# A graph network's first layer: ScalarE's and TensorE's inputs to a batch's tables are placed earlier, VectorE's readings of them later

## The reference, cut to what matters

```python
# N = 6250 nodes, 206250 edges (src, dst) sorted by dst, x is 6250 x 128
def _mean_agg(x, src, dst, n):
    msg_sum = segment_sum(x[src], dst, num_segments=n)
    cnt = segment_sum(ones, dst, num_segments=n)
    return msg_sum / maximum(cnt, 1.0)
def _sage_conv(x, src, dst, Wl, bl, Wr):
    return _mean_agg(x, src, dst, n) @ Wl.T + bl + x @ Wr.T
h = maximum(layernorm(x), 0)
h = relu(batch_norm(_sage_conv(h, ..., Wl0, bl0, Wr0)))   # 128 -> 256, "layer 0"
h = relu(batch_norm(_sage_conv(h, ..., Wl1, bl1, Wr1)))   # 256 -> 256, "layer 1"
h = log_softmax(_sage_conv(h, ..., Wl2, bl2, Wr2))        # 256 -> 128, "layer 2"
return x + h
```

## Time and profile before

| | us |
|---|---|
| median of 3 runs | 1572.43 (1569.44 to 1576.12) |
| the profiled execution | 1564.77 |
| its span in the trace | 1563.0 |
| mean granted TensorE clock in it | 0.953 |
| TensorE busy (matmuls) | 1338.6 |
| VectorE / ScalarE / GpSimd busy | 597.6 / 524.1 / 575.3 |

### The profile page before, as it was taken

One profiled execution on the slowest core, in us unless ns is written; L12 is line 12 of the kernel. 1 busy time (PEld: TensorE's weight loads), 2 busy tenths in 40 slices (PEclk: granted clock), 3 DMA queues, 4 the chain that ended last, 5 costly groups with the idle time before them and its releaser, 6 DMA issues.

```text
span 1563.0 us, 36182 instructions
## 1 busy us (share of the span) xinstructions
PE 1338.6 (86%) x16035; PEld 872.4 (56%) x16035; DVE 597.6 (38%) x1108; ACT 524.1 (34%) x848; POOL 575.3 (37%) x586
## 2 busy tenths in 40 slices
PE   1467787768777678899999999999999899999997
PEld 1366676657666667776544444444444774444445
DVE  6966656656476667521201111110210321212213
ACT  4875675657656557634200000000000150000001
POOL 4323132140221310000066666666666004666650
PEclk9988988889899989999999999999999999999999
DMA  5243434352524424413666666676664369888993
GB/s 156 89 160 123 169 112 167 104 182 87 190 103 173 180 89 178 168 40 130 211 227 211 222 213 220 211 241 232 204 228 150 86 207 315 319 300 308 330 320 103
DMA packets 92007, 291.45 MB, mean 186 GB/s; under 512 B 17538, under 2 KB 53012, under 8 KB 88612
## 3 DMA queue, kind: packets, MB, share of 16 engines
q1 hardware_dynamic: 63596, 228.73, 40.9%
q0 software_dynamic: 21824, 55.44, 11.6%
q10 hardware_dynamic: 6424, 4.88, 1.0%
HBM read 197.78 MB, written 91.22 MB: 185 GB/s over the span
## 4 chain that ended last, share of the span: by engine, by line
PE 66%; DVE 10%; issue 9%; POOL 6%; DMA 4%; ACT 4%; ACTq 0%; DVEq 0%; SPq 0%; POOLq 0%
PE bank L1638 25%; PE bank L1215 12%; PE cells L1638 12%; PE cells L1205 4%; DVE hots L889 3%; PE bank L1883 3%; DVE parts L889 2%; DMA hots<-table,src_i 2%; POOL hots L519 2%; PE cells L1250 2%; PE cells L1704 2%; PE bank L1641 2%; ACT junk L606 2%; POOL parts L482 2%; POOL parts L492 1%
## 5 line engine op out<-in xcount | busy, mean ns | idle before, releaser
L519 POOL DMA_INDIRECT hots<-table,src_i x444 | 420.6, 947 | 440.9 <-DMA table<-parts 206.1
L1638 PE MATMUL bank<-ring,parts 128*128 128x500 f16 x2058 | 461.4, 374 | 0.0
L1215 PE MATMUL bank<-ring,parts 64*128 64x250 f16 x4900 | 346.5, 285 | 115.9 <-DVE agm L900 112.1
L658 ACT CAST ring<-cells 128x980 f16<-128x980 f32 (+1 forms) x325 | 337.6, 1054 | 210.1 <-PE cells L1205 203.8
L1215 PEld LDWEIGHTS bank<-ring,parts 64*128 64x128 f16 x4900 | 249.7, 100 | 140.4 <-issue 118.7
L1638 PEld LDWEIGHTS bank<-ring,parts 128*128 128x128 f16 x2058 | 192.3, 96 | 224.8 <-issue 11.3
L1638 PE MATMUL cells<-ring,parts 128*128 128x500 f16 (+1 forms) x980 | 215.9, 373 | 0.0
L889 DVE TENSOR_TENSOR hots<-iotas,tab 128x2560 f16<-128x2560 f16 (+1 forms) x210 | 198.5, 1002 | 9.5 <-ACT tab L622 8.2
L729 ACT ACTIVATE agmg<-cells,isp 128x124 f32<-128x124 f32 x20 | 7.3, 365 | 470.0 <-PE cells L1259 470.0
L1638 PEld LDWEIGHTS cells<-ring,parts 128*128 128x128 f16 (+1 forms) x980 | 90.9, 96 | 112.7 <-issue 9.0
L889 DVE TENSOR_TENSOR parts<-iotas,tab 128x2560 f16<-128x2560 f16 (+3 forms) x140 | 134.5, 1013 | 9.8 <-ACT tab L622 5.8
(11 more groups left out here) (213 smaller groups left out, 1030.8 us busy)
## 6 DMA issues: line engine op xcount, KB each, us to landing
ring<-c_blocks SPq DMA_DIRECT2D x120, 750.0 KB, 5.9
c_blocks<-ring SPq DMA_DIRECT2D x25, 3062.5 KB
ring<-c_blocks SPq DMA_DIRECT2D x40, 812.5 KB, 7.2
rcb<-rc_row SPq DMA_DIRECT2D x69, 125.0 KB
hots<-table,src_i POOLq DMA_INDIRECT x444
Z<-in_x_dram SPq DMA_DIRECT2D x4, 768.0 KB, 6.1
table<-parts SPq DMA_DIRECT2D x2, 1536.0 KB
table<-parts ACTq DMA_DIRECT2D x2, 1536.0 KB
```

Source lines behind the costliest of these rows:

```text
L519: pool.indirect_dma_start(out=got[layer][:, 5 * (r % NGOT) + i, :], out_offset=None, in_=tables[layer], in_offset=bass.IndirectOffsetOnAxi ...
L658: act.copy(blk[c % 2][:, :, :].rearrange("p a (d g) -> p a d g", d=GD)[:, :, :, GPS * i:GPS * i + n], cells[t % 2][:, :, 0:n * NA].rearran ...
L1215: ins = pe.matmul(bank[2 + h][:, 0:BD], small[rows, a, part, :], blk[c % 2][rows, a, :], start=(a, part) == (0, 0), stop=(a, part) == (FUL ...
L1638: ins = pe.matmul(bank[b][:, 0:2 * BD].rearrange("p (s d) -> p s d", s=2), lhs, ring[0:r, :, BD * a:BD * a + BD], start=(a, part) == (0, 0 ...
```

## The change

It moves chores to other steps of the dictionary, splits "ends" in two ("firsts" is TensorE's small matmul, "ends" is what VectorE and POOL do), and moves VectorE's statistics of a block from step i = 6 to i = 11 (last blocks excepted). The tables of batch 2, made while batch 1 runs, keep their old places but for "ends", one step later on VectorE and POOL. No instruction is added or dropped, and buffers are as they were.

```diff
@@ -75,17 +75,22 @@
         chores[5 + k] = ("shift", 1, c)
         chores[12 + k] = ("turn", 1, c)
     chores.update({3: ("ends", 1, 0), 9: ("tile", 1, 0), 10: ("place", 1, 0), 11: ("table", 1, 0)})
+
     for q in range(1, len(batches)):
         t0 = NST * batches[q][0]
-        chores[t0 + 9] = ("count", q, 0)
+        at = {"sample": 1, "count": 9, "rows": 12, "row": 14, "firsts": 19, "windows": 25, "ends": 27, "shift": 34, "tile": 38,
+              "place": 39, "table": 45, "turn": 46}
+        if q == 1:
+            at = {"count": 9, "sample": 11, "rows": 18, "row": 24, "windows": 31, "firsts": 33, "ends": 34, "shift": 37, "tile": 41,
+                  "place": 42, "table": 46, "turn": 48}
+        chores[t0 + at["count"]] = ("count", q, 0)
         if q + 1 < len(batches):
             for k, c in enumerate(range(*batches[q + 1])):
-                chores[t0 + 11 + k] = ("sample", q + 1, c)
-                chores[t0 + 24 + k] = ("row", q + 1, c)
-                chores[t0 + 37 + k] = ("shift", q + 1, c)
-                chores[t0 + 48 + k] = ("turn", q + 1, c)
-            chores.update({t0 + 18: ("rows", q + 1, 0), t0 + 31: ("windows", q + 1, 0), t0 + 33: ("ends", q + 1, 0), t0 + 41: ("tile", q + 1, 0),
-                           t0 + 42: ("place", q + 1, 0), t0 + 46: ("table", q + 1, 0)})
+                for what in ("sample", "row", "shift", "turn"):
+                    chores[t0 + at[what] + k] = (what, q + 1, c)
+            for what in ("rows", "windows", "firsts", "ends", "tile", "place", "table"):
+                chores[t0 + at[what]] = (what, q + 1, 0)
+    chores[2] = ("firsts", 1, 0)
 
 
     table_at = {t + k: (k, chores[t][1]) for t in list(chores) if chores[t][0] == "table" for k in ((-2, -1, 0) if chores[t][1] > 1 else (0,))}
@@ -1116,7 +1121,7 @@
                         dve_table(table_at[t][1], table_at[t][0], own)
                     if c >= 2 and i == 6:
                         dve_sums0(c - 2, own)
-                    b = made0.get((c, i - 6))
+                    b = made0.get((c, i - (11 if c < NB else 6)))
                     if b is not None:
                         dve_stats(0, b)
                     if c == NB and i == 2:
@@ -1171,7 +1176,7 @@
 
         def ends_before(c):
 
-            return 1 + sum(what == "ends" and t < turn_step.get(c, 0) for t, (what, _, _) in chores.items())
+            return 1 + sum(what == "firsts" and t < turn_step.get(c, 0) for t, (what, _, _) in chores.items())
 
         def pe_turn(q, c):
             k = c - batches[q][0]
@@ -1304,7 +1309,7 @@
                     what, q, b = chores.get(t, ("", 0, 0))
                     if what == "turn":
                         pe_turn(q, b)
-                    elif what == "ends":
+                    elif what == "firsts":
                         pe_ends(q, 1 + sum(w == "turn" and k < t for k, (w, _, _) in chores.items()))
                     if c >= 1:
                         if i == 1:
```

## The result

The changed kernel took 1532.02 us (median of 4 runs, 1520.86 to 1536.32) against 1573.45 of the kernel before on the same chip (1569.44 to 1576.12): a ratio of 0.9728 with the interval [0.9667, 0.9789]. It is faster by 41 us where the forecast said 70; the range held it, the forecast's middle did not. Its profiled execution took 1528.2 (span 1526.5).

A forecast was written before the change was run, and what follows sets the result against it. No engine is full; VectorE, ScalarE and TensorE wait for each other in turn. Gains of 92.4 + 26 + 6.6 = 125 us less 30, 18, 2 and 5 back gave 70: 1572.4 - 70 = 1502 us, range 1466 to 1545.

The forecast's parts named there:

- the lead: VectorE's steps ahead of ScalarE or TensorE: at most 4 or 0 before, 6 to 9 after; TensorE needs five at i = 1.
- one-hot waits: At VectorE's ends TensorE runs out of one-hots, 1.31 us once a batch; 6.6 us over five batches to be gained.
- the ring: Layer 0's engines wait in turn: VectorE at statistics 88.3, rows 29.8, windows 18.8, ends 18.7 us, then TensorE 92.4.
- VectorE's longest blocks: Last block of a batch: about 18.5 us of VectorE work, no stop expected; norms in blocks 20 and 21 cost 5 us.
- the new wait: TensorE's small matmul at step 19 waits for VectorE's step 25: about 0.5 us, 2 us over four batches.
- The slower rival: VectorE only four steps ahead at TensorE's step 19, so TensorE stops: 32 us in all, 1604 us; chance 0.04.
- TensorE's pauses: Instruction supply falls behind during the 3 MB store; 14 blocks losing their stop get 2.6 us each, 30 us taken.
- rival "all of it": Pauses belong to something else and ScalarE's chores fit between: 30 + 10 us more gained, 1462 to 1472; chance 0.17.
- ScalarE's chores: Samples and rows, 7.5 us a batch, now all stand in the open at steps 1 to 4 and 14 to 17: 18 us.
- the slow matmuls: After each stop TensorE's sums run at 1.2 GHz, 1.86 us lost; some 14 stops from block 6 on, 26 us gained.
- what moves at no cost: Shifts, tile, count and POOL's place, covered by VectorE's remaining slack of some 3 us a block; no cost booked.
- The rival on VectorE and POOL: Gather issues beside VectorE's builds take longer, the table is late, TensorE stops: 28 us back, 1530 us; chance 0.17.

The follow-up runs named there:

- paced kernel: Changed kernel, single store, each gather of windows and ends of batches 3 to 6 made to wait for one more ScalarE cast: 0.9585, 1495.17 us.
- split store: Changed kernel with each block's 3 MB store issued in four parts at steps 0, 3, 6 and 9 of the next block: 0.9412, again 0.9404.
- quarter store: Changed kernel storing only the last quarter of each block's counts, which the loads of layers 1 and 2 read four times: 0.9454.
- best version: Changed kernel with the store in four parts and the gathers tied to ScalarE's casts, both together: 0.9393, 1465.12 us.

## Why the prediction was right, and where it was off

**Right: what bounds the kernel, and the lead.** The stops were forecast to fall from 92.4 to under 20 and fell to 12.6; the statistics' waits from 88.3 to under 15, and fell to 12.1. The one-hot waits, 6.6 us forecast, are gone altogether (9.0 us of them before). From block to block the batches of the paced kernel, which has no crawl, last 84.0, 87.4, 82.6 and 88.4 us, where 82 to 88 were forecast.

**Wrong: the statistics as part of the ring.** The forecast counted their 88.3 us, the largest wait of all, among those that take the lead away, and gave each rendezvous a lead of five or more. With the statistics left where they were (a lead of four) VectorE waits 97.9 us there and the time is 0.9661, no worse than the whole change; moved by themselves they gave 0.9974. Between two versions without a crawl, 0.9661 and the paced 0.9585, their move is worth 12 us of some 65. It is the chores that had to move.

**Right by luck: VectorE's longest blocks.** Ahead of blocks 20 and 21, with the norms, TensorE stops for 3.65 and 2.59 us; 5 were forecast, 6.2 measured. But the same kernel's second profile has 8.17 and 2.57, and the paced kernel 8.43 and 2.56. That one also stops 3.41, 2.77 and 3.81 us ahead of blocks 8, 12 and 16, the last of their batches, where no stop was expected: 21.0 us in all. The term was too low by 16 us, and a crawl earlier in the batch can hide it.

**Right and too high: the new wait.** TensorE waited once for "firsts", 0.4 us, where 2 were put down. The slower rival hung on this place, and nothing of it came. It does show up in the two versions with the statistics at i = 6, 3.9 and 11.3 us, and with 1.6 or 1.7 in three others: the lead is there, with little to spare.

**Right in mechanism, too high in idle: TensorE's pauses.** Thirty us of idle were forecast. By the count above the pauses grew from 15.5 to 31.3 us, by 15.8; the other 11.2 us of idle with no releaser are the crawl's. Splitting the store gave back 30.05 us, more than the idle; the slow clock behind the pauses, which the forecast had not put down to them, is a likely part of that. That they belong to the store is shown by three edits (split, a quarter, split on the kernel before). That it is the supply of instructions is what the count of packets says; no run changed the supply itself. The rival "all of it", with its rule of the Trainium skill ("Runtime: NRT & Kernel Launch", "Instruction fetch mechanics") that the crossings are mostly hidden, falls: here most are hidden until a 3 MB store is under way.

**Too high in idle: ScalarE's chores.** Forecast 18 us. The row that shows it, TensorE waiting for ScalarE's cast, is 10.5 us (0.3 before). No run took the chores away by themselves, so what else they cost stays open.

**Off: the slow matmuls, 26 us.** This term came in only in part, and the crawl is the main reason. Busy time from 160 to 600 us, columns as above; first the kernel before:

```profile
160.00:600.00 440.00, 330.23 (x8007) 292.89 (x8009) 277.82 (x424) 277.93 (x357) 94.31 (x76) 0.89 0.39 145
```

The changed kernel:

```profile
160.00:600.00 440.00, 375.52 (x9027) 321.31 (x9025) 320.77 (x479) 311.12 (x400) 128.09 (x87) 0.91 0.44 158
```

The same with paced gathers:

```profile
160.00:600.00 440.00, 376.15 (x9418) 330.44 (x9414) 323.70 (x496) 320.67 (x408) 138.68 (x88) 0.95 0.46 169
```

With only two levels, 1.2 and 2.4 GHz, a mean of 0.89 is 97 us at the lower one, 0.91 is 79 and 0.95 is 44. Where nothing crawls, then, 53 us fewer are slow, which is about 26 us of time: the term as it was forecast. I booked the slow clock as something that stops at i = 1 bring. TensorE also falls to 0.50 in a crawl (all of 199 to 209 us above), so in the changed kernel the slow stretches moved rather than went.

**Wrong: nothing new was to come on POOL.** The forecast said that POOL's groups of gathers "each move six steps forward with VectorE's part", listed under what moves at no cost. Before, "ends" had to wait for TensorE, the four gathers of "windows" and the four of "ends" stood apart, and TensorE stood still for VectorE near them. Now they come in one row of eight beside an engine that works, and in three blocks TensorE, ScalarE and VectorE all fell to a fraction of their pace, 29 us by the blocks' lengths, 22 to 32 by pacing. No term of the sum stands for this. Without it the change stands at 0.9585 [0.9543, 0.9628]; the forecast, 1502 of 1572.4, is 0.955. So the crawl has the size of what was missed. That the rest agrees so well is partly luck: the idle of the pauses and of ScalarE's chores was forecast too high by some 22 us, the stops at VectorE's longest blocks too low by 16. And the range held the result because it was wide, not because anything in it foresaw the crawl.

**The rival on VectorE and POOL** had nearly the time (1530), and the changed kernel owes that time to something else, the crawl. Of the rival's mechanism it has one case: in batch 4 the last shifts come late, and TensorE stops ahead of block 16. VectorE's and then TensorE's row in the timeline of the changed kernel:

```profile
405.43 0.29 DVE L779 TENSOR_SCALAR parts<-parts,cf 128x128 f32<-128x128 int32 x1 [2.84 <-DMA parts<-in_pairs_dram,last_i]
...
421.69 1.85 PE L1220 MATMUL bank<-ring,parts 64*128 64x250 f16 x16 [5.52 <-DVE agm L905]
```

That is 5.5 us once, and in the very batch that did not crawl. It returns where the crawl is gone: in the split store's two profiles VectorE stands idle ahead of shifts in all four batches, 13.0 and 9.3 us, in the paced kernel 24.4 (there the pacing itself makes gathers late), and stops of 0.6 to 8.4 us ahead of blocks 8, 12, 16 or 20 follow. The profile gives most of these waits no releaser; by the code the shift waits for the gathers to land. How much of the stops is theirs and how much the longest blocks' work was not told apart. In the crawl the gathers' issues are not long but short: 0.94 us each, while VectorE, itself held up, builds nothing. Beside builds, in the split store's block 6, the first three took 2.06, 1.80 and 1.88 us.

**What stays open.** Why a row of gathers slows TensorE at all. It is not the number of gathers, nor TensorE's clock: the version without the statistics' move issues eight in a row too, begins three of its four rows at 0.50 and does not crawl, the split store's do not in two profiles, and the quarter store's crawl with the clock at 0.95 and more in the rows of gathers. Nor is it the lack of instructions of the pauses, by the count. That gathers have a part in it is shown from two sides: by the paced kernel, and by where TensorE's idle places off the count of 193 lie. The five profiles that show a crawl (two of the changed kernel) have 129 of them from 160 to 720 us, all during rows of gathers or less than 1.5 us behind; the other eight, the kernel before among them, have none. In the crawls most issues took 0.94 us and followed each other at 1.25; in the quiet groups builds of VectorE stretched more of them, to between 1.2 and 2.3. That could feed itself: short issues, late releases, no builds, short issues. No run tested it. Holding some gathers back ended the crawl, but so did splitting the store without touching them (not so with the statistics back at i = 6), and what the two have in common is not known. Nor is it settled why the versions differ in who crawls; and of the 125 us of gross gain the best version has 93 (1557.97 to 1465.12).

## What to carry to other kernels

Where two engines meet at several places in a batch, taking away the largest wait moves it to the next place; so look for the places with the smallest lead, not for the longest wait, and try each half of such a change alone: here the longest wait could have stayed. A stop also hides things: price what now stands in its shadow (a store, a row of gathers) before booking the whole stop as won, and expect edits there that were worth nothing to be worth tens of us afterwards. Try spreading a large store over the steps of the next block, and holding back gathers that would otherwise follow one another at once, and judge such parts in the combination that will be kept: here two that were each good alone made 0.9874 together.

## What the chip showed that was not expected

- While POOL issued eight gathers in a row, TensorE's matmuls came in batches of about five every 0.73 us, and ScalarE and VectorE stood idle for up to 5.5 and 6.5 us until a release by nothing in the profile. It did not come with every such row; with gathers tied to casts it was gone in all four batches, and in the changed kernel with the store split too.
- With a store of 3 MB in one piece a packet of TensorE's instructions came 9.0 us behind the one before, and TensorE paused for up to 3.2 us, always 193 instructions behind a multiple of 256. With the same bytes in four pieces the longest pause was 1.6 us in one profile and 2.4 in another.
